# Two levels of the fifteen-addition product over four batches, in a float32 kernel with low-rank terms

## What is computed

```
x1 = x  + (x  @ B_b^T) @ A_b^T            # first adapter
y  = x1 + x1 @ W + (x1 @ lora_A_b) @ lora_B_b
```

## Time and profile before

| | us |
|---|---|
| median of 3 runs (1401.36 to 1405.29) | 1402.17 |
| the profiled execution | 1402.34 |
| its span | 1400.7 |
| PE busy | 1367.2 |
| DVE busy | 810.2 |
| ACT busy | 405.9 |
| POOL busy | 165.0 |

### The profile page before, as it was taken

The page is one execution under the profiler, slowest core; times in us unless marked ns, Lnnn a source line. Parts: engine busy times, 40 slices in busy tenths (PEclk is TensorE's granted clock), DMA queues, the critical chain, the costliest instruction groups (busy, mean ns, idle before and its releaser), DMA issues.

```text
span 1400.7 us, 15653 instructions
## 1 busy us (share of the span) xinstructions
PE 1367.2 (98%) x6016; PEld 1129.2 (81%) x6016; DVE 810.2 (58%) x941; ACT 405.9 (29%) x462; POOL 165.0 (12%) x317
## 2 busy tenths in 40 slices
PE   5999999999999999999999999999999999999997
PEld 4888888888878888888887888888887888888886
DVE  3455855357776455646775555555766445554675
ACT  2332222223234223322332323232322422232230
POOL 3200100111123010012011010012012001001202
PEclk8999999999999999999999999999999999999999
DMA  8864843458887343357684252446785334234755
GB/s 303 310 225 134 299 158 113 153 186 280 294 280 240 122 136 120 129 195 246 236 289 146 86 173 96 151 151 213 256 297 187 99 120 135 91 91 133 223 201 180
DMA packets 76778, 261.81 MB, mean 187 GB/s; under 512 B 12176, under 2 KB 12176, under 8 KB 76576
## 3 DMA queue, kind: packets, MB, share of 16 engines
q1 hardware_dynamic: 57600, 205.55, 43.5%
q0 software_dynamic: 19104, 55.27, 11.7%
HBM read 213.52 MB, written 48.30 MB: 187 GB/s over the span
## 4 chain that ended last, share of the span: by engine, by line
PE 85%; DVE 5%; DMA 5%; ACT 2%; issue 2%; POOL 0%; POOLq 0%; SPq 0%; ACTq 0%; DVEq 0%
PE y_ps L1024 76%; PE lr_ps L955 4%; PE p_ps L997 3%; DMA w_raw<-in_W 2%; PE y_ps L976 2%; ACT w_hi L555 2%; DVE w_lo L708 1%; DVE w_raw L694 1%; DVE b_lo L721 1%; DMA w_raw<-w_sum 1%; DVE u L776 1%; DMA stage_all<-lrw 0%; DMA u<-in_A0n 0%; DVE u L777 0%; DVE val L835 0%
## 5 line engine op out<-in xcount | busy, mean ns | idle before, releaser
L1024 PE MATMUL y_ps<-b_hi,w_hi 128*128 128x512 f32 x1792 | 699.3, 390 | 15.3 <-DVE w_lo L708 8.8
L1024 PE MATMUL y_ps<-b_lo,w_hi 128*128 128x512 f32 x1792 | 698.6, 390 | 0.0
L1024 PE MATMUL y_ps<-b_hi,w_lo 128*128 128x512 f32 x1792 | 698.4, 390 | 0.0
L708 DVE TENSOR_TENSOR w_lo<-w_raw,w_hi 128x1024 fp32r<-128x1024 f32 x216 | 264.6, 1225 | 460.9 <-ACT w_hi L555 460.9
L555 ACT CAST w_hi<-w_raw 128x1024 fp32r<-128x1024 f32 x216 | 227.6, 1054 | 879.5 <-PE y_ps L1024 474.9
L1024 PEld LDWEIGHTS y_ps<-b_hi,w_hi 128*128 128x128 f32 x1792 | 337.3, 188 | 86.6 <-DVE w_lo L708 8.8
L1024 PEld LDWEIGHTS y_ps<-b_hi,w_lo 128*128 128x128 f32 x1792 | 337.2, 188 | 70.2
L1024 PEld LDWEIGHTS y_ps<-b_lo,w_hi 128*128 128x128 f32 x1792 | 337.3, 188 | 70.1
L721 DVE TENSOR_TENSOR b_lo<-x_raw,b_hi 128x1024 fp32r<-128x1024 f32 x112 | 136.5, 1219 | 0.0
L566 ACT CAST b_hi<-x_raw 128x1024 fp32r<-128x1024 f32 x112 | 117.5, 1049 | 2.4 <-DMA x_raw<-in_xT 2.4
L694 DVE TENSOR_TENSOR w_raw<-w_raw 128x1024 f32<-128x1024 f32 x64 | 78.1, 1221 | 19.5 <-DMA w_raw<-in_W 11.6
(11 more groups left out here) (81 smaller groups left out, 605.8 us busy)
## 6 DMA issues: line engine op xcount, KB each, us to landing
w_raw<-in_W SPq DMA_DIRECT2D x208, 512.0 KB, 3.8
w_raw<-w_sum SPq DMA_DIRECT2D x96, 512.0 KB, 3.6
x_raw<-in_xT SPq DMA_DIRECT2D x64, 512.0 KB, 5.4
out_y<-u POOLq DMA_DIRECT2D x64, 256.0 KB, 6.4
out_y<-stage_all POOLq DMA_DIRECT2D x64, 256.0 KB, 3.4
lr_raw<-lrw POOLq DMA_DIRECT2D x64, 128.0 KB, 4.0
w_sum<-w_raw SPq DMA_DIRECT2D x8, 512.0 KB, 6.2
c_kept<-stage_all POOLq DMA_DIRECT2D x16, 256.0 KB, 3.2
```

What stands on the lines that cost most here:

```text
L708: dve.tensor_tensor(w_lo[n % 2][:, :, :], w_tile(n)[:, :, :], w_hi[n % 2][:, :, :].bitcast(F32), ALU.subtract).then_inc(w_ready, 1)
L1024: last = pe.matmul(bank[:, :], w[n % 2][:, c, t * P:(t + 1) * P], x[:, 2 * j + c, :], start=(j == 0 and c == 0 and w is w_hi and x is b_hi ...
```

## The change

The scheme is used at two levels. Four batches (two pairs) make a "quad", of which there are two. The outer level has seven products M1, M2, M6, M7, M4, M3, M5 (in this order) of a quad, the inner level seven products Q1, Q2, Q6, Q5, Q7, Q3, Q4 of each outer one, so there are 98 inner products. Each is a 512 x 512 block of weights by a 512 x 512 block of x: two units of two column tiles each, four chunks of rows, three matmuls. A unit has 24 matmuls, as before, and an outer product has 14 units (u = 0 to 13). Below, M2/0 is outer product M2 of the first quad, M2/1 that of the second.

- **Operands.** Each outer product has four weight blocks (`wq`) and four x blocks (`xq`) in SBUF. In M6, M4 and M5 the x blocks are first-level differences (`xq` sums: two halves of 1024 elements each), in M6, M3 and M5 the weight blocks are first-level sums (`wq` sums). In each outer product four differences of x (t1 to t4) and, in the first quad, four sums of weights (s1 to s4) of 2048 elements are formed in place. For the second quad all weight operands are read from HBM (`w_ops`), where SP stored them during the first.
- **The third buffer set.** Second operands, and partial results that are read back, come through three tiles `tmp` of 1024 elements, used in one fixed order (`tmp_plan`) and loaded by POOL. M7's operands are differences that are needed long before M7: they are formed in M1/0 for the weights (`s3p`) and in M2/0 and M2/1 for x (`t3p`), eight times each, one per unit at u = 5 to 12, from two `tmp` tiles into the first of them, and stored to HBM from there.
- **PSUM.** Q1, Q6, Q7, Q4 accumulate in the same four banks one after another; Q2, Q5, Q3 use two banks in turn. Partial results go to `u2`, to `stage`, and for M7 through HBM (`u3_kept`).
- **Low-rank terms.** For batches 0 to 3 and for 4 and 5 results are stored without them, and read back, completed and stored again in 48 units of the second quad (`fixes`): ACT copies a tile to `p_ps` (`seed`), PE adds one matmul, ACT copies it back (`fixed_copy`). For batches 6 and 7 they are added in `fin` in M5/1. The products for `p_ps` take 256 columns instead of 512.
- **Lookahead.** As before, iteration n of DVE and ACT splits the weights of unit n + 1 after PE's unit n - 1 (`unit_free`).

The diff, cut to its core (new lines, and the old ones that they replace; the steps of iteration n run on DVE in this order: evicts part 0, early sums, `w_split(n + 1)`, `x_split`, evicts part 1, `fin`, late sums, splits of adapters and low-rank factors):

```diff
-P1, P2, P6, P7, P4, P3, P5 = range(7)
-PRODUCTS, UNITS = 7, 8
+M1, M2, M6, M7, M4, M3, M5 = range(7)
+Q1, Q2, Q6, Q5, Q7, Q3, Q4 = range(7)
+UNITS = 14
+PRODUCTS = 49
+CHAIN = (Q1, Q6, Q7, Q4)
...
+    TMPS = 3
...
+    def late_sums(n):
...
+            if u == 8 and x_worked(nmo):
+                out.append(("xq", nk, nmo, 0))
+            if u == 10 and x_worked(nmo):
+                out.append(("xq", nk, nmo, 2))
+            if u == 12 and x_worked(nmo):
+                out.append(("xq", nk, nmo, 3))
+            if u == 13:
+                out.append(("t3", nk, nmo))
+            if nk == 0:
+                if u == 9 and w_worked(nmo, 0):
+                    out.append(("wq", nmo, 0))
+                if u == 11 and w_worked(nmo, 2):
+                    out.append(("wq", nmo, 2))
+                if u == 12:
+                    out.append(("s3", nmo))
+                if u == 13 and w_worked(nmo, 1):
+                    out.append(("wq", nmo, 1))
...
+            if u == 0 and n and w_worked(mo, 3):
+                out.append(("wq", mo, 3))
...
+            if mo == M1 and 5 <= u < 13:
+                out.append(("s3p", *divmod(u - 5, 2)))
+        if mo == M2 and 5 <= u < 13:
+            out.append(("t3p", k, (C11, C12, C22, C21)[(u - 5) // 2], (u - 5) % 2))
...
+            if key[0] in ("s3p", "t3p"):
+                use_tmp(n, 1, key[0] + "a", *key[1:])
+                use_tmp(n, 1, key[0] + "b", *key[1:])
...
+            def load_tmp(e):
+                key = tmp_plan[e]
+                kind, slot = key[0], e % TMPS
+                if e >= TMPS:
+                    pool.wait_ge(*tmp_free(tmp_plan[e - TMPS]))
...
+                pool.dma_start(tmp[slot][:, :, :].rearrange("p s n -> p (s n)"), src.rearrange("p a b -> p (a b)")
+                               ).then_inc(tmp_loaded[slot], 16)
...
+                for e in tmp_uses.get((n, 1), []):
+                    kind, *key = tmp_plan[e]
+                    if kind in ("s3pa", "t3pa"):
+                        continue
+                    after = [e]
+                    if kind in ("s3pb", "t3pb"):
+                        store_kept(kind[:3], *key)
+                        after = [e - 1, e]
+                    if kind == "u3":
+                        store_fin(*finish(n))
+                    for f in after:
+                        if f + TMPS < len(tmp_plan):
+                            load_tmp(f + TMPS)
...
+            def kept_sum(kind, *key):
...
+                a, b = tmp_tile((kind + "a", *key)), tmp_tile((kind + "b", *key))
+                dve.wait_ge(*tmp_here((kind + "a", *key)))
+                dve.wait_ge(*tmp_here((kind + "b", *key)))
+                last = dve.tensor_tensor(a[:, :, :], a[:, :, :], b[:, :, :], ALU.subtract)
...
+                last.then_inc(kept_summed, 1)
...
+                sums(early_sums(n))
+                if n + 1 < LAST:
+                    w_split(n + 1)
+                if n // 2 + 1 < LAST // 2:
+                    x_split(n // 2 + 1, n % 2)
...
+                if finish(n):
+                    fin(*finish(n))
+                sums(late_sums(n))
...
+            def seed(n, t):
+                act.wait_ge(fix_loaded[fix_no[n] % 2], 16 * (fix_no[n] // 2 + 1))
...
+                act.copy(p_ps, fix_tile[fix_no[n] % 2][:, t, :]).then_inc(seeded, 1)
...
+            def p_mm(mo, po, h):
...
+                        last = pe.matmul(p_ps[:, h * N // 2:(h + 1) * N // 2], a0[:, 4 * kg + c, :], w[:, h, c, :],
...
+                    for c in range(4):
+                        for i, (w, b) in enumerate(((w_hi, b_hi), (w_hi, b_lo), (w_lo, b_hi))):
+                            last = pe.matmul(out, w[:, h, c, col:col + P], b[x],
```

More of the change, by code:

```diff
@@ new lines, in product, with by_act @@
+    def product(q):
+        return q // 49, q // 7 % 7, q % 7
+    def by_act(q, first):
+        return first and product(q)[1] in (M1, M5)
+    fixes = {}
+    for mo, pair, own, quarters in ((M1, 0, 0, (0, 1)), (M2, 0, 0, (2, 3)), (M6, 1, 0, (0, 1)), (M7, 1, 0, (2, 3)),
+                                    (M4, 0, 1, (0, 1)), (M3, 0, 1, (2, 3))):
+        for i, u in enumerate((3, 4, 6, 7, 9, 10, 12, 13)):
+            fixes[unit(1, mo, u)] = (batch(own, pair, i // 2 % 2), 4 * quarters[i // 4] + 2 * (i % 2))
@@ new lines, in lora_residual_program, with use_tmp @@
+    lr_split_of = {i: n for n, uses in lr_split_at.items() for i in uses}
+    lr_mms = {}
+    for n in range(LAST + 1):
+        if n in fixes:
+            for t in range(2):
+                lr_mms["fix", n, t] = len(lr_mms) + 1
+        end = finish(n)
+        if end and end[0]:
+            for which in (1, 0):
+                for t in range(2):
+                    lr_mms["fin", end[1], end[2], which, t] = len(lr_mms) + 1
+    tmp_plan, tmp_when = [], []
+    def use_tmp(n, late, *key):
+        tmp_plan.append(key)
+        tmp_when.append((n, late))
@@ new lines, in lora_residual_program, with stage_stores @@
+    for n in range(LAST + 1):
+        if finish(n):
+            fin_no[finish(n)] = len(fin_no) + 1
+    def stage_stores(m, c, h):
+        uses = stage_uses[GROUP[m % 7][c], h]
+        return sum(o % 7 != M5 for o, _ in uses[:uses.index((m, c)) + 1])
+    in_no, in_at = {}, {}
+    order = []
+    for k in range(QUADS):
+        for mo in IN_OF:
+            base = unit(k, mo, 0)
+            order += [(max(base - 2, -1), k, mo, Q1), (base + 2, k, mo, Q2), (base + 6, k, mo, Q7),
+                      (base + 10, k, mo, Q3)]
@@ new lines, in product_free, with quarter_done, added_before @@
+        def product_free(q):
+            waits = [(tile_done, 4 * q + 4)]
+            if product(q) in in_mm_no:
+                waits.append((in_mm_done, in_mm_no[product(q)]))
+            return waits
+        def quarter_done(k, mo, c, t):
+            po = LAST_OF[c]
+            return evicted(product_at(k, mo, po), 2 * (t // 2) if po in CHAIN else t, c)
+        def added_before(q, t, count, c, first):
+            k, mo, po = product(q)
+            if not first:
+                before = max(o for o in ADDS if o < po and c in [d for d, _ in ADDS[o]])
+                return evicted(product_at(k, mo, before), 2 * (t // 2) if before in CHAIN else t + count - 1, c)
+            base = {M2: M1, M6: M1, M7: M6, M3: M6}.get(mo)
+            return None if base is None else quarter_done(k, base, c, t + count - 1)
@@ new lines, in lora_residual_program, with bank_of @@
+        p_reads, p_read = {}, {}
+        adds = copies = 0
+        for mo, po in p_no:
+            p_reads[mo, po] = {Q1: (0, 1), Q2: (0,)}.get(po, (1,))
+            if po == Q1 and mo in (M1, M4):
+                copies += 1
+                p_read[mo, po] = p_copied, copies
+            else:
+                adds += len(p_reads[mo, po])
+                p_read[mo, po] = p_added, adds
+        def bank_of(q, t, count):
+            if q % 7 in CHAIN:
+                return ps[:, t:t + count, :]
+            return r_ps[r_at["tile", q, t] % 2]
@@ new lines, in g_mm @@
+            def g_mm(kh):
+                r = r_at["g", kh]
+                for pair in r_free(r - 2):
+                    pe.wait_ge(*pair)
+                pe.wait_ge(a0_ready, kh + 1)
+                pe.wait_ge(a1_ready, kh + 1)
+                for c in range(HC):
+                    for i, (a0, a1) in enumerate(((a0_hi, a1_hi), (a0_hi, a1_lo), (a0_lo, a1_hi))):
+                        last = pe.matmul(r_ps[r % 2][:, 0:P], a0[:, c, :], a1[:, c, :], start=(c == 0 and i == 0),
+                                         stop=(c == HC - 1 and i == 2))
+                last.then_inc(g_mm_done, 1)
```

1951 lines of the change are left out of this document (1152 added, 799 removed).

## The result

The changed kernel takes 1634.59 us (median of 4 runs, 1628.53 to 1639.08), the kernel before 1401.76 (4 runs). The ratio is 1.1653, with a 95% interval of 1.1608 to 1.1698. I had forecast 1507, slower by 7%. The direction was right, the size was less than half of what came, and the time lies outside the range (1400 to 1590).

What follows compares the result with a forecast made beforehand. Kernel bound by TensorE; PE's work 1210 us, plus start 34, end 15, chain of kept differences 203 and DVE's excess 43, gives a 1505 us span, 1507 in all, 7% slower; range 1400 to 1590.

Steps and rivals of the forecast that it cites:

- PE's work: TensorE's matmul time over the whole changed kernel: 1210 us, 148 less than before.
- the kept differences: M1/0, M2/0, M2/1: store, reload and difference wait for one another without cover; 203 us including work behind M2.
- the rest: Everything beyond PE's work and the kept differences: start 34, end 15, DVE's excess over PE 43 us.
- reloads and DVE's load behind M2: After the chains in M2/0 and M2/1: tile reloads and units of DVE's load, 21 and 7 us.
- my rivals: Whole kernel: short transfers 1403 us (chance 0.13), chain covered 1325 (0.08), transfers grown longer 1618 (0.11).
- The readback: Second quad's low-rank terms: four ACT copies a unit, covered by PE, no cost; uncovered, 2 us in 48 units.
- The start: Beginning of the kernel: waits for 16 transfers of x and W and for adapters, 34 us (30 to 40).
- M5/1 and the end: Last stage: DVE's excess over PE 14 us, then the last `fin` after PE's last tile 15 us.
- PE's clock: In the stalls PE restarts at 1.2 GHz; units with added matmuls cost some 8 us, left to the range.
- The short-transfer rival: Chain of kept differences with S 3.0 and L 3.6 us costs 112 us, 1403 in all; chance 0.13.
- S: Landing time of the 512 KB store of a kept difference from `tmp`: taken as 5.0 us.
- L: Landing time of a 512 KB load into `tmp`: taken as 5.0 us.

Runs made afterwards that it cites:

- experiment 1: Changed kernel without the kept differences (s3p, t3p), operands read from W and x unchanged: 1463.05 us.
- experiment 5: Changed kernel without both the kept differences and the loads and stores of the readback: 1405.64 us.
- experiment 11: experiment 5 plus earlier A0 splits, earlier split of joined values, and the adapter product's store before POOL's wait for a landing: 1372.41 us.
- the swap: Changed kernel with each kept difference written into the second tile of its pair instead of the first: 1592.86 us.
- Experiment 12: experiment 11 with inner differences of x and three inner sums of weights covering only 256 or 512 of 2048 elements: 1341.98 us.
- experiment 9: experiment 8 with the next load issued right behind the store that frees its tile, and ACT's first seed behind its splits: 1634.83 us.
- experiment 8: Changed kernel with the readback's loads and stores issued by SP instead of POOL: 1600.94 us.

## Why the prediction was right and wrong

By leaving parts out in turn, the span of 1626.9 goes to 1461.1, 1403.9 and 1370.8 (experiments 1, 5, 11), and PE's work is 1210. That splits the 417 us over PE's work into 166 for the kept differences, 57 for the readback's transfers, 33 for the small waits and 161 for the rest. My sum had 203, 0, 0 and 92 for the four, of which 28 of the 203 were reloads and DVE's load behind M2, which experiment 1 leaves in place. With those counted to the rest, it is 175, 0, 0 and 120, in all 295. So of the 122 us that were missing 57 are the readback, 41 the rest and 33 the small waits, and the kept differences gave 9 back. The readback's cost is what puts the time outside the range: without its transfers the kernel took 1561 us, inside 1400 to 1590. None of my rivals was this case. The split depends on the order in which parts are left out, and each step is a single execution.

- **PE's work.** 1210 us for 5544 matmuls held: stages without waits took PE's time to about 1 us, M2/1 86.3 for 87.1 by my count in experiment 11. The products of 256 columns started 120 ns apart by the median, the value that I had picked between two rows.
- **The kept differences.** Right in mechanism, place and size: 175 forecast, 166 measured. Units with a second sum took 19.0 to 21.4 us in M2/0 (forecast 19.5), those with one difference 15.0 in M2/1 and mostly 10 to 12 in M1/0 (12.6). The two landings that I took as equal, 5.0 each, were 3.1 and 6.5 to 6.8 by their medians; in M2/1, where the readback's transfers run beside it, the store took 5.1 and the load of x 7.3. That the two errors cancel was luck. With a shorter store there was less for the swap to gain than I had expected.
- **The readback: the step that failed.** "The readback of the first batches' low-rank terms costs ACT four copies ... no cost" looked at ACT's busy time and not at when the tile comes. It named a price if the copies weren't covered (2 us in each of 48 units) and left it out of the range; but the copies were not what cost. A tile is stored and loaded again between two uses, and with two tiles and 1.5 units a use on average that is the same turn as in `tmp`, which I had worked out in the paragraph before. I had counted the traffic of these transfers but not their round trip. It cost 57 us by itself and 74 beside the chain.
- **Small waits.** The gathers of adapters on POOL, 8 blocks at 1.2 us, and the join's PSUM bank, which is freed only at the end of DVE's next iteration, weren't in the sum: 33 us. The start of the kernel before showed the price of such a gather in its own wait for adapters.
- **The rest.** The start was better than forecast: 14 us to the first unit and M1/0 within 7 us of PE's work in experiment 11, together 21 for 34. M5/1 and the end cost 38 for 29. The first quad from M2/0 to M5/0 and the first units of M1/1 and M6/1 cost about 102 for 57. DVE's load was less than I had counted (M2/0 97 us for 105, M4/0 78 for 86), so the excess can't be more work of DVE. Experiment 12 gives part of the 102 to DVE's load; how the remainder divides between single reloads of `tmp` and POOL's queue wasn't taken apart.
- **PE's clock.** The granted clock was 0.81 in M2/0, where PE idles between units, and 0.98 there without the chain. It adds to PE's busy time (109.5 us for 97 of work), but the turn of `tmp` alone fills the units of 20 us. The rule that I cited from the Trainium skill (TensorE: Matmul & The Clock Gate, section HAM oscillation) agrees with that fall, 0.81 against 0.98. By the starts in the trace 318 matmuls of the changed kernel came some 454 ns apart, the pace of the lower level of the clock (1.2 GHz), together 64 us beyond full pace, against 24 us in experiment 11. No run here separates how much of that lies on the path: that it is small is not shown.
- **The short-transfer rival.** An estimate from the page DMA: Bandwidth & Descriptors of the Trainium skill, section Anatomy of one DMA, was 3.2 us for 512 KB. The store of the kept difference has it, 3.1 by the median; the loads into `tmp`, at 6.0 to 7.3, are twice that at a mean share of 0.71. So S came out as in this rival and L above my 5.0; the rival needed both.

## What to carry to other kernels

Fewer matmuls are worth something only as far as every buffer's round trip fits in the shorter loop: for each buffer that is stored and loaded again, add up compute, issue, store landing and load landing, divide by the number of buffers, and hold that against the units between uses, whichever engine waits at its end. Do it for all such buffers, not only the one that looks worst. A wait for a landing holds up whatever its queue issues next: in experiment 9 that was the store of the other buffer, and all of experiment 8's gain was lost again.

## What the runs showed that I had not expected

Landings of 512 KB differ widely in one kernel, at a mean share of 0.71, and not by direction alone. By the medians, POOL's loads into `tmp` took 6.0 to 7.3 us and SP's loads mostly 5.6 to 6.7. POOL's stores from `tmp` to `t_kept`, `w_ops` and `out_y` took 3.1 to 3.2, but those from `tmp` to `c_kept` 5.9 and those from `stage` to `c_kept` 8.2:

```profile
c_kept<-tmp POOLq DMA_DIRECT2D x8, 512.0 KB, 5.9
out_y<-tmp POOLq DMA_DIRECT2D x8, 512.0 KB, 3.2
```

In the kernel before, loads of that size took 5.0 at a share of 0.80; the changed kernel's are longer at the same or lower share, and the runs don't say why.
